# Cross-attention stage of a Perceiver layer: the product of queries and key weights moves to the end of each step, and the first tile's preparations change places

## What is computed

```
x = x + xattn(layernorm(x), ctx)   # 16 heads of 64; 64 sequences: 64 queries, 256 keys each
x = x + attn(layernorm(x))         # causal self-attention over 64 rows, 16 heads of 64
x = x + ffn(layernorm(x))          # 8 experts, top 2, 256 -> 512 -> 256
# xattn:
q, k, v = x @ Wq, ctx @ Wk, ctx @ Wv             # x: 4096 x 256; ctx: 16384 x 192
attn = softmax(q k^T / 8) ; out = (attn v) @ Wo + bo
```

## Time and profile before

| | |
|---|---|
| median of 3 runs | 2470.9 us (2468.84 to 2471.3) |
| profiled execution | 2464.55 us, span 2462.8 us |
| busy share of the span | TensorE 91%, its weight loads 81%, VectorE 65%, ScalarE 52%, GpSimd 34% |
| mean granted TensorE clock | 0.974 of full speed |
| the first stage | up to about 1365 us of the span |
| TensorE waits for the copy of turned probabilities | 1.0 us before a turn and 0.9 us before a product with values, once each |
| TensorE waits for the rest of the output (`ot_lo`) | 0.9 us, once |

### The profile page before, as it was taken

The page is one execution under the profiler, slowest core; times in us unless marked ns, Lnnn a source line. Parts: engine busy times, 40 slices in busy tenths (PEclk is TensorE's granted clock), DMA queues, the critical chain, the costliest instruction groups (busy, mean ns, idle before and its releaser), DMA issues. The chain is left out here.

```text
span 2462.8 us, 55962 instructions
## 1 busy us (share of the span) xinstructions
PE 2246.8 (91%) x18992; PEld 2002.1 (81%) x18992; DVE 1602.1 (65%) x3655; ACT 1290.3 (52%) x3906; POOL 842.3 (34%) x1022
## 2 busy tenths in 40 slices
PE   7999999999999999999999699999999984999996
PEld 6888888888888888888888599999999972888885
DVE  6666656665656565656565688898898857545442
ACT  4554555455545454555454466666667640445442
POOL 2332333332323333333323222222222230667664
PEclk8999999999999999999999899999999995999998
DMA  3000000000000000000000400000000011433434
GB/s 109 18 19 13 21 24 18 9 26 17 26 9 26 17 26 9 26 17 26 9 13 6 146 10 10 17 17 9 17 17 9 18 44 37 97 78 77 102 53 103
DMA packets 61946, 82.52 MB, mean 34 GB/s; under 512 B 9936, under 2 KB 45520, under 8 KB 61808
## 3 DMA queue, kind: packets, MB, share of 16 engines
q1 hardware_dynamic: 48912, 63.46, 8.1%
q0 software_dynamic: 12960, 18.12, 4.4%
HBM read 59.80 MB, written 25.96 MB: 35 GB/s over the span
## 5 line engine op out<-in xcount | busy, mean ns | idle before, releaser
L411 POOL TENSOR_TENSOR p_sb<-p_sb,rinv 128x512 f32<-128x512 f32 x256 | 279.0, 1090 | 906.9 <-DVE rinv L760 906.9
L668 ACT ACTIVATE p_sb<-s_ps,nmax 128x256 f32<-128x256 f32 x512 | 238.1, 470 | 282.0 <-DVE nmax L735 278.8
L757 DVE COPY pt_sb<-t_ps 128x512 f32<-128x512 f32 x256 | 176.9, 691 | 191.4 <-PE t_ps L554 190.7
L918 POOL TENSOR_TENSOR sp_sb<-sp_sb,srinv 128x512 f32<-128x512 f32 x128 | 133.1, 1040 | 426.2 <-DVE srinv L1112 426.2
L735 DVE TENSOR_REDUCE nmax<-s_ps 128x2 f32<-128x512 f32 x256 | 176.4, 689 | 156.8 <-PE s_ps L65 155.2
L65 PE MATMUL qk_ps<-q_sb,wkt_hi 128*128 128x256 f32 x496 | 142.4, 309 | 102.8 <-DVE qk_hi L57 95.2
L65 PEld LDWEIGHTS qk_ps<-q_sb,wkt_hi 128*128 128x128 f32 x496 | 93.6, 189 | 165.8 <-DVE qk_hi L57 135.6
L1060 ACT ACTIVATE sp_sb<-sm_sb,snmax 128x128 f32<-128x128 f32 x512 | 199.4, 390 | 7.2 <-DVE snmax L1123 4.1
L46 ACT ACTIVATE q_sb<-m_ps 64x256 fp32r<-64x256 f32 x256 | 96.8, 378 | 195.2 <-PE m_ps L65 189.5
L45 ACT CAST qk_hi<-qk_ps 128x512 fp32r<-128x512 f32 x248 | 147.3, 594 | 70.9 <-PE qk_ps L65 65.2
L65 PE MATMUL s_ps<-cx_hi,qk_hi 128*128 128x256 f32 x512 | 165.3, 323 | 2.2 <-issue 2.2
(11 more groups left out here) (293 smaller groups left out, 7569.8 us busy)
## 6 DMA issues: line engine op xcount, KB each, us to landing
ctx_raw<-in_ctx_t SPq DMA_DIRECT2D x32, 256.0 KB, 2.8
ctx_raw<-in_ctx_t SPq DMA_DIRECT2D x64, 128.0 KB, 2.9
x_ring<-in_x SPq DMA_DIRECT2D x16, 256.0 KB, 2.8
x_mid<-x_ring SPq DMA_DIRECT2D x16, 256.0 KB, 2.2
xn<-f_xn SPq DMA_DIRECT2D x16, 256.0 KB, 2.2
acc<-x_sb SPq DMA_DIRECT2D x16, 256.0 KB, 2.3
e_raw<-in_gate SPq DMA_DIRECT2D x8, 512.0 KB, 3.9
e_raw<-in_up SPq DMA_DIRECT2D x8, 512.0 KB, 4.8
```

What stands on the lines that cost most here:

```text
L411: nc.gpsimd.tensor_tensor(prob, prob, inv, ALU.mult).then_inc(norm_done, 1)
L668: ex = nc.scalar.activation(p_sb[:, k, b * J:(b + 1) * J], s_ps[1 - w][:, b * J:(b + 1) * J], ACT.Exp, bias=nmax[:, k, b:b + 1], scale=1.0 ...
L757: nc.vector.tensor_copy(pt_sb[:, (p - 3) % 4, :], t_ps[:]).then_inc(t_done, 1)
L918: nc.gpsimd.tensor_tensor(prob, prob, inv, ALU.mult).then_inc(norm_done, 1)
```

## The change

In all tiles but the first, a late product goes to the very end of the step on TensorE, and an early one behind the values. ScalarE's and VectorE's copies follow. In the prologue x is turned before any key weights, the value weights are split before the first queries are copied, the identity products shrink from 128x128 on 16 columns to 16x16 on 16 columns of output, and layernorm of the second group moves from steps 0, 1 and 2 of the first tile to 3, 4 and 5.

```diff
 # GpSimd, tile
-                        if u == 0 and p == 1 and look:
+                        if u == 0 and p == (4 if first else 1) and look:
                             ln_rstd(pool, ln, t // 2 + 1)
...
 # TensorE, tile
                             if EARLY_WK + p < PAIRS:
                                 turn_wk(EARLY_WK + p)
-                        elif early is not None:
-                            absorb(*early[:3], two_banks=False)
...
                             values(n, u, p)
-                        if late is not None and not first:
-                            absorb(*late[:3], two_banks=False)
+                        if early is not None and not first:
+                            absorb(*early[:3], two_banks=False)
...
+                        if late is not None and not first:
+                            absorb(*late[:3], two_banks=False)
 
                 pe.wait_ge(s_const, CONSTS)
                 for _ in range(WARM):
-                    pe.matmul(y_ps[:, 0:16], ident[:], ident[:, 0:16], start=True, stop=True)
-                turn_wk(0)
+                    pe.matmul(y_ps[0:16, 0:16], ident[:, 0:16], ident[:, 0:16], start=True, stop=True)
                 turn_x(0)
-                for pair in range(1, EARLY_WK):
+                for pair in range(EARLY_WK):
                     turn_wk(pair)
...
 # ScalarE, tile
-                        if early is not None:
-                            absorbed_hi(*early, two_banks=first)
+                        behind = unit_behind(t, u, p, first, look, drain)
+                        if behind is not None:
+                            absorbed_hi(*behind, two_banks=False)
                         if first:
+                            absorbed_hi(*early, two_banks=True)
                             absorbed_hi(*late, two_banks=True)
...
                         if first:
-                            for i in ((Q_SPLIT, Q_SPLIT + 1) if p == 0 else (V_SPLIT + p - 1,) if p < 3 else ()):
-                                weights.split_hi(act, i)
+                            if 1 <= p < 3:
+                                weights.split_hi(act, V_SPLIT + p - 1)
...
-                        if late is not None and not first:
-                            absorbed_hi(*late, two_banks=False)
+                        if early is not None and not first:
+                            absorbed_hi(*early, two_banks=False)
...
-                wk_hi_copy(0)
                 xt_hi_copy(0)
-                for pair in range(1, EARLY_WK):
+                for pair in range(EARLY_WK):
                     wk_hi_copy(pair)
-                for n in range(Q_SPLIT):
+                for n in range(V_SPLIT):
                     weights.split_hi(act, n)
 # VectorE, tile
-                        elif early is not None:
-                            absorbed_lo(*early[:3], two_banks=False)
                         if proj is not None:
                             q_lo(*proj)
-                        if first and p == 0:
-                            split_wv()
-                            rem_lo(0, 0)
+                        if early is not None and not first:
+                            absorbed_lo(*early[:3], two_banks=False)
...
-                        if p == 0 and u == 0 and look:
+                        if p == (3 if first else 0) and u == 0 and look:
...
-                        if p == 2 and u == 0 and look:
+                        if p == (5 if first else 2) and u == 0 and look:
...
-                def split_wv():
-                    weights.split_lo(dve, Q_SPLIT)
+                def split_wv_rem():
...
-                wk_lo_copy(0)
                 xt_lo_copy(0)
-                for pair in range(1, EARLY_WK):
+                for pair in range(EARLY_WK):
                     wk_lo_copy(pair)
-                for n in range(Q_SPLIT):
+                for n in range(Q_SPLIT + 1):
                     weights.split_lo(dve, n)
+                rem_lo(0, 0)
                 q_lo(0, 0)
+                split_wv_rem()
```

## The result

The changed kernel takes 2363.6 us (2362.28 to 2363.8, 4 runs) against 2469.9 (2466.5 to 2471.3, 4 runs) in the same comparison: ratio 0.957, 95% interval 0.955 to 0.959. Forecast: 2373, inside its own range. The two profiled executions are 2464.55 and 2363.80, 100.8 apart, where 97 were forecast.

A forecast was written before the change was run, and what follows sets the result against it. TensorE, 91% busy, was taken as the bound, idling 8.4 us per 83.0 us period. Steady steps 94 plus prologue 3 gain 97; set against the 2470.9 median, that gave 2373 us, range 2352 to 2398 (own range 2362 to 2384).

The forecast's parts named there:

- The mechanism: Steady steps: the subtraction stays 1.72 us behind the scores' end; moving products only changes when TensorE asks for it.
- Waits left, 2.0 a period: TensorE, steady steps: 0.75 + 0.55 + 0.13 + 0.20 and four restarts of 0.10 remain of 8.4 us.
- TensorE's own work, 74.6 a period, and four restarts of 0.10: Priced pieces of 16 steps sum to 74.6 of 83.0 us; the first matmul behind a wait costs 0.10 more.
- Layernorm just fits: Steady layernorm steps: subtraction delays of 0.85 and 1.05 us fit the following odd step's spare of 1.06.
- The delay of 1.05: VectorE, steady steps: layernorm's application puts the subtraction 1.44 - 0.39 = 1.05 us later.
- The rival of 2400: VectorE too late at the layernorm steps: waits of 0.85 and 1.05 stay, 27 us lost, 2400; chance 0.09.
- New waits do not appear: Steady steps: engines shift against each other, all 8.4 us a period gained, 30 us more, 2343; chance 0.06.
- Slower: End-of-step product stalls, delaying the next scores and step chain; at 2.0 us late, 86 slower, 2556; chance 0.03.
- Prologue, 3: Prologue and first tile: 2.6 us gained, between -0.5 and 4; taken as 3.
- 0.8 + 2.2 - 0.4: First projection 0.8 us earlier, step 1's scores' wait of 2.2 gone, layernorm's new place costing 0.4.
- The baseline: Forecast set against the median of 2470.9 us, 6.3 above the profiled 2464.55, from which 2367.5 would follow.

The follow-up runs named there:

- e9: e8 with the second and third query projection of an odd tile one step later (3 and 5 instead of 2 and 4); 2352.5 us, ratio to before 0.952.
- e4: Changed kernel with late products left behind the values, as before the change; 2518.8 us, ratio to before 1.021.
- e8: Changed kernel with one product each in odd steps 1 to 7 and even steps 0 to 6, both tiles' second one in step 4; 2374.6 us.
- p3: Changed kernel with two more 128x512 additions on VectorE before layernorm's application in step 2 of even tiles; 2384.4 us, ratio to before 0.965.
- e7: Changed kernel with the edits of e5 and e6 together; 2342.4 us, ratio to before 0.948.
- e2: Changed kernel with the products moved back, so only the prologue and first-tile edits remain; 2464.2 us, ratio to before 0.998.
- e5: Changed kernel with step 1's first product back behind the scores, its copies before those of the queries; 2352.1 us, ratio to before 0.952.
- e3: Changed kernel with the two early products of an odd tile (steps 1 and 3) left behind the scores; 2369.2 us, ratio to before 0.960.
- e6: Changed kernel with an odd tile's double step at 4, with the output projection between the two products, instead of 3; 2354.8 us, ratio to before 0.953.
- e1: Kernel before with only the products moved, prologue and first tile as before; 2365.1 us, ratio to before 0.958.
- p1: Changed kernel with the second group's layernorm in steps 0, 1 and 2 of the first tile as before; 2362.6 us, one run.

## Why the forecast held, point by point

- *The mechanism*: right. Where no layernorm and no second product is in front, the subtraction lets the product start 1.72 behind the scores' end, as before (624.39 to 626.11; 621.77 to 623.49 in e9); what was changed is when TensorE asks. The changed kernel's own period came 0.4 under the forecast. Of the ten periods of the experiments, worked out before their runs from the measured 76.2 or 83.0, six came within 0.2 us; the other four (e4, e8, e9, p3) were off by a cause that the trace then named.
- *Waits left, 2.0 a period*: 0.78, 0.55, 0.13 found where 0.75, 0.55, 0.13 stood. At step 6 of an even tile 0.20 fits too: product at 604.11, values at 602.38, 604.11 - 602.38 - 1.17 - 0.35 = 0.21.
- *TensorE's own work, 74.6 a period, and four restarts of 0.10*: 0.5 too much together. e7 runs at 74.6 with step 6's 0.2 left, so the work is 74.4. A product behind the turn of the probabilities or the product with values takes 0.57 to its successor, not 0.48, with a wait in front (618.63 to 619.21) or without (589.22 to 589.79), and the scores behind it take 1.20 (589.79 to 590.99), not 1.29. So only step 3's first product, behind the values, has a restart on top (626.11 to 626.69). The period is then 74.4 + 0.78 + 0.55 + 0.13 + 0.21 + 0.10 = 76.2, and the gain 6.8 instead of 6.4.
- *Layernorm just fits*: the application fits with 0.47 to spare, not 0.01. The delay of 1.05 did not carry over: with the product between turn and scores, the copy of turned probabilities and layernorm start earlier against the scores (585.89 against scores at 585.25, 0.64; before, 1.17). The rival of 2400 rested on this; p3 shows that with more than half a microsecond more on VectorE the product at step 3 does wait.
- *New waits do not appear* (2343): wrong, the waits of steps 1 and 3 are there; e7 shows that this time is to be had, but by other edits.
- *Slower*, by a stalled product at the step's end: nothing of it. e4 shows the nearest case, a product that stalls 2.24 once a period, though behind another product and not at the step's end: 3.1 a period slower than before, 0.7 of it the clock.
- *Prologue, 3*: between the profiles compared it is 2.6, but of other parts than 0.8 + 2.2 - 0.4: the first projection comes 0.2 earlier (22.10 to 21.86), step 1's scores 3.6 (35.00 to 31.36), so that 1.0 is lost again by the turn. The wait in front of step 1's scores went, as put. Over ten profiles the turn is at 71.6 on average, 4.7 earlier: the four with the clock up from step 1's scores on (e2 to e5) have 69.1 to 70.6, the other six 72.1 to 74.2, so the 4.5 of e2 and the 3 of the forecast both lie inside what the clock moves. What the new place of layernorm costs was not told apart. I had the first key weights start 1.2 earlier; they start at 11.36, since in this execution GpSimd's doubling began at 10.55, not 10.02.
- *The baseline*: I set the gain against the median, 6.3 above the profiled execution (the sum 2470.9 - 97 is 2374, not 2373). This is the larger part of the error: of the 9.4 by which 2363.6 lies under 2373, 5.5 were put on there (2373 - 2367.5), and only 3.8 are the change's. At 2464.55 the profiled execution of before is faster than every other run of that kernel on record (2466.0 to 2475.7). The third stage's instructions are the same in all profiles, yet from its first expert product to the end of the span it takes 2462.8 - 2089.1 = 373.7 in the profile of before, 374.3 in that of the changed kernel, and up to 383.5 in e8:

```profile
L65 PE MATMUL e_g_ps<-e_w_hi,e_xt_hi x134: 391/475/775, 1998.3 to 2351.4; 128*128 128x512 f32 x134
```

(span 2381.8). The profile of before has the shortest third stage of the 14. So executions differ by several us in a stage that the change leaves alone; the periods do not. e3, e6, e7 and p3, whose medians are 4 to 6 over, have 377.5 to 379.9 there. Why that stage varies is open.

The parts between the profiles: first tile 2.6 (3 forecast), 14 periods 96.0 (90), from the last turn to the second stage 3.6 (4.5), later stages -1.4 (0): 100.8.

## What to carry to other kernels

When an engine waits for a buffer that others empty, work out when it comes free and when it is asked for, both from the same event, and move the asking to where the gap closes; moving the products was free here, with each queue's order following: e1's period is the one worked out. Look at every buffer that the moved instruction reads, not only the one that it waits for: e8 lost 2.2 us a period against e7 (76.8 and 74.6), 1.5 of it at step 2 and 0.6 at step 4, to the release of its input. Judge such edits by a period inside the profile; here it settled what medians a few us apart could not.

## What the runs showed of the hardware

- Narrow identity products (16 columns of weights): 48 passes in 1.46 us, 0.030 each, against 10.43 us, 0.217 each, with 128 columns of weights. The Trainium skill (TensorE: Matmul & The Clock Gate, section Back-to-back issue gap) gives about 25 ns from start to start as the floor, or about 62 ns where instructions are decoded in software; the trace, with 30 ns, is near the first and far under the second.
- In the 13 periods of e4 the clock fell six times behind a step's waits, in 3 of 13 cases of a single 2.24 and in 3 of 13 of 0.39 and 1.57 close together, each time for 1.5 us of loss; what sets those cases apart is open. In the kernel before, with single waits up to 1.56, and in p3 (1.51) it never fell between 150 and 1230 us (granted clock 1.00). The Trainium skill (TensorE: Matmul & The Clock Gate, section What's actually happening) says that the clock is throttled by default and that activity releases it; the trace agrees, as e4's granted clock is 0.66 from 598 to 603, behind the wait, and 1.00 from 603 to 608, when TensorE had been at work again since 598.15.
- In one and the same prologue the moment when products go from 0.21 to 0.12 apart varies from launch to launch. In the changed kernel's profile it rises, falls in the middle of step 1's scores (0.12 apart at 31.36, 0.21 from 31.79 on), is up again at 35.12, and products are 0.21 apart once more between 45.3 and 48.5; in e2's the same scores run at full speed. With full speed there and after (e2 to e5), first projection to turn takes 49.4, otherwise 50.5 to 52.0.
- The profile's granted clock doesn't fit the rows there: p1 and p3 show 1.00 from 30 to 35 while their step 1 scores, ten products, take 2.33, as at half speed (1.36 in e2's profile, at full speed).
